# The LayerNorm apply of the QKV stage goes from GpSimd with four input slots to VectorE with two

## What is computed

```
q, k, v = ln(x) @ Wq.T, ln(x) @ Wk.T, ln(x) @ Wv.T      # 2048, 512, 512 columns; 8 kv heads, 4 queries each
a_dot   = softmax(q k^T / 8) v                            # 32 heads of 64
a_mem   = elu(q) @ memory / (elu(q) @ memory_norm)
out     = a_dot * (1 - w) + a_mem * w                     # w = sigmoid(memory_weight)
ffn(x)  = ((silu(ln(x) @ w_gate * s_gate) * (ln(x) @ w_up * s_up)) @ w_down) * s_down   # int8 weights, 8192 inner
ln(x)   = (x - mean(x)) / sqrt(var(x) + 1e-5)
```

## Time and profile before

| | us |
|---|---|
| runs shown (2): median | 3299.47 |
| runs shown: lowest, highest | 3222.3, 3376.64 |
| the profiled execution, device time | 3150.48 |
| its span on the slowest core (4) | 3148.8 |
| spans of the eight cores | 3109.7 to 3148.8 |

### The profile page before, as it was taken

How to read it: one execution, slowest core, us unless ns; L and a number is a source line. 1 busy time by engine, 2 the same in 40 slices (tenths; PEclk the granted TensorE clock), 3 DMA queues, 4 the chain that set the end, 5 groups by cost and what they waited for, 6 DMA issues and landing times.

```text
span 3148.8 us, 40986 instructions; the slowest of 8 cores (3109.7 to 3148.8 us)
## 1 busy us (share of the span) xinstructions
PE 2460.3 (78%) x14265; PEld 1331.1 (42%) x14265; DVE 594.8 (19%) x1657; ACT 963.0 (31%) x1671; POOL 590.8 (19%) x1071
## 2 busy tenths in 40 slices
PE   3677667787844699968999778786449997899986
PEld 1232222122211477724777322221127775278752
DVE  1323332111136300020000011112460002010010
ACT  2200030899930122201222049996002221022210
POOL 1100010000000133323333310000003332333333
PEclk8788867788855799989999988887559998999999
DMA  5222113000000499979999970000009997999999
GB/s 142 71 43 47 38 59 84 23 4 4 3 2 1 151 360 355 359 274 360 356 351 356 354 255 4 4 4 3 1 1 360 355 350 251 395 352 361 346 332 346
DMA packets 161916, 591.77 MB, mean 188 GB/s; under 512 B 20920, under 2 KB 23096, under 8 KB 157368
## 3 DMA queue, kind: packets, MB, share of 16 engines
q0 software_dynamic: 151344, 552.14, 51.2%
q1 hardware_dynamic: 10376, 37.01, 3.4%
HBM read 325.23 MB, written 8.39 MB: 106 GB/s over the span
## 4 chain that ended last, share of the span: by engine, by line
PE 58%; DVE 12%; ACT 11%; DMA 11%; issue 8%; DVEq 1%; SPq 0%; POOL 0%; ACTq 0%; POOLq 0%
PE pAB L713 14%; PE pAB L704 14%; ACT arena L481 9%; DMA warena<-wd 8%; PE pCD L296 5%; PE pAB L296 5%; PE pCD L675 3%; PE pE L493 3%; PE pAB L461 3%; PE pF L493 2%; PE pAB L578 2%; PE pF L675 2%; PE pE L675 2%; PE pT L238 2%; DVE x L633 1%
## 5 line engine op out<-in xcount | busy, mean ns | idle before, releaser
L704 PE MATMUL pAB<-ln_fm,warena 128*128 128x256 bf16 x4096 | 493.5, 274 | 9.7 <-DMA warena<-wg 4.8
L713 PE MATMUL pAB<-ln_fm,warena 128*128 128x256 bf16 x4096 | 490.1, 273 | 9.9 <-DMA warena<-wu 6.3
L694 POOL DMA_DIRECT2D warena<-wg x256 | 136.2, 532 | 1733.6 <-PE pAB L704 1038.7
L704 PEld LDWEIGHTS pAB<-ln_fm,warena 128*128 128x128 bf16 x4096 | 398.0, 98 | 122.5 <-issue 39.1
L713 PEld LDWEIGHTS pAB<-ln_fm,warena 128*128 128x128 bf16 x4096 | 399.0, 98 | 63.6 <-issue 16.4
L481 ACT ACTIVATE arena<-pAB,bias_s 128x512 bf16<-128x512 f32 x512 | 372.0, 727 | 48.2 <-PE pCD L468 44.9
L481 ACT ACTIVATE arena<-pCD,bias_s 128x512 bf16<-128x512 f32 x512 | 374.3, 731 | 0.0
L461 PE MATMUL pAB<-q_fm,k_fm 64*128 64x512 bf16 x512 | 219.7, 439 | 131.7 <-ACT arena L481 126.7
L720 ACT ACTIVATE gtmp<-pAB,sg_s 128x256 bf16<-128x256 f32 x256 | 121.2, 473 | 566.0 <-PE pAB L713 505.2
L728 DVE TENSOR_TENSOR arena<-gtmp,utmp 128x256 bf16<-128x256 bf16 x256 | 74.8, 292 | 1061.7 <-ACT utmp L724 1061.7
L493 PE MATMUL pE<-arena,v_tm 128*65 128x512 bf16 x512 | 230.3, 450 | 0.0
(11 more groups left out here) (121 smaller groups left out, 2070.1 us busy)
## 6 DMA issues: line engine op xcount, KB each, us to landing
warena<-wd POOLq DMA_DIRECT2D x512, 512.0 KB, 6.0
warena<-wg POOLq DMA_DIRECT2D x256, 512.0 KB, 3.8
warena<-wu POOLq DMA_DIRECT2D x256, 512.0 KB, 4.7
x<-x SPq DMA_DIRECT2D x16, 1024.0 KB, 7.0
xstage<-x SPq DMA_DIRECT2D x8, 1024.0 KB, 5.0
warena<-wqt POOLq DMA_DIRECT2D x16, 512.0 KB, 5.2
y<-x SPq DMA_DIRECT2D x8, 1024.0 KB, 5.2
warena<-wkt POOLq DMA_DIRECT2D x8, 512.0 KB, 5.2
```

What stands on the lines that cost most here:

```text
L704: ttg = P.do("t", lambda e, it=it, wb=wb, c=c: e.matmul(pA[0:128, 0:256], wgb[wb][:, c, :], ln2_fm[:, c, 0:256], start=(c == 0), stop=(c = ...
L713: ttu = P.do("t", lambda e, it=it, wb=wb, c=c: e.matmul(pB[0:128, 0:256], wub[wb][:, c, :], ln2_fm[:, c, 0:256], start=(c == 0), stop=(c = ...
```

## The change

The apply of the QKV stage is issued on VectorE instead of GpSimd; the four input slots become the two halves of `xstage`; the waits of the later reloads of `x1` that guarded the two borrowed slots go. Places in the order of emission stay: stats(i), tail(i-1), apply(i). In the VectorE queue the apply of tile i thus stands behind V copy(i-1) and ahead of stats(i+1).

```diff
-        xslots = [xstage[:, 0, :], xstage[:, 1, :], x1[:, 2, :], x1[:, 3, :]]
-        xstreams = ["xs0", "xs1", "a2", "a3"]
-        war_xslot = [None] * 4
         for H in range(2):
             for i8 in range(8):
                 i = H * 8 + i8
                 sl = i % 2
-                s4 = i % 4
-                t_x[i] = P.do("y", lambda e, i=i, s4=s4: e.dma_start(
-                    out=xslots[s4], in_=x_d[i * 128:(i + 1) * 128, :]),
-                    waits=[war_xslot[s4]], stream=xstreams[s4])
-                tv3 = emit_ln_stats(xslots[s4], sl, [t_x[i]], war_lnst[sl],
+                t_x[i] = P.do("y", lambda e, i=i, sl=sl: e.dma_start(
+                    out=xstage[:, sl, :], in_=x_d[i * 128:(i + 1) * 128, :]),
+                    waits=[war_xstage[sl]], stream="xs%d" % sl)
+                tv3 = emit_ln_stats(xstage[:, sl, :], sl, [t_x[i]], war_lnst[sl],
                                     sum_on_s=True)
                 if i8 > 0:
                     emit_tile_tail(i - 1)
-                t_apply[i] = emit_ln_apply(xslots[s4], sl, tv3, eng="g")
-                war_xslot[s4] = t_apply[i]
+                t_apply[i] = emit_ln_apply(xstage[:, sl, :], sl, tv3, eng="v")
+                war_xstage[sl] = t_apply[i]
             emit_tile_tail(H * 8 + 7)
...
         t_sdb = P.do("y", lambda e: e.dma_start(out=xstage[:, 1, :], in_=sdb_d[:]),
-                     waits=[war_xslot[1]], stream="xs1")
+                     waits=[war_xstage[1]], stream="xs1")
...
-                xw = [t_y[loc]] if p == 1 else []
-                if p == 0:
-                    if loc == 0:
-                        xw = [P.lastj]
-                    elif loc >= 2:
-                        xw = [t_apply[12 + loc], war_lnst[loc % 2]]
                 t_x1.append(P.do("y", lambda e, p=p, loc=loc: e.dma_start(
                     out=x1[:, loc, :],
                     in_=x_d[p * 512 + loc * 128: p * 512 + (loc + 1) * 128, :]),
-                    waits=xw, stream="a%d" % loc))
+                    waits=[t_y[loc]] if p == 1 else
+                          ([P.lastj] if loc == 0 else []), stream="a%d" % loc))
```

## The result

| | before | after |
|---|---|---|
| median, us | 3145.38 (10 runs) | 3162.67 (11 runs) |
| lowest, highest, us | 3135.86, 3376.64 | 3157.5, 3403.88 |
| ratio | | 1.0067 (95% interval 1.0047 to 1.0086) |
| the profiled execution's span, slowest core | 3148.8 | 3176.4 |
| mean span of the eight cores, same execution | 3131.1 | 3158.8 |

A program on all eight cores has a second state in which a die runs at a lower granted clock; the two runs shown with the kernel before (3222.3 and 3376.64) were both in it, and the ratio leaves such runs out.

What follows compares the result with a forecast made beforehand. VectorE and TensorE taking turns on one chain was taken to bound the QKV stage. Exposed applies 21.5 plus head 2.4 gave 23.9, near 24 us; on the shown median 3299.5 that made 3323.5, range 3165 to 3400.

Steps and rivals of the forecast that it cites:

- The time stated: Whole kernel: 3323.5 us, from the shown runs' median 3299.5 plus 24; range 3165 to 3400.
- The middle tiles: QKV stage, six tiles a half: the apply exposed behind the V copy costs 1.45 us each, 12 times.
- The last tiles: Last tile of each half: no stats hide the first transposes, so copies start 2.05 us later, twice.
- The first tile of a half free: First apply of each half costs nothing: VectorE idles 3.9 us behind it for ScalarE's sums, against 1.35.
- Sum of the exposed applies: Both halves of the QKV stage: 12 x 1.45 + 2 x 2.05 = 21.5 us.
- The head: Start of the kernel: two earlier Q loads beside the first x loads delay it 2.4 us, bounds 0 and 5.
- The slots: x loads with two input slots instead of four: cost nothing, with about 11 us before VectorE feels a late load.
- Rival C: QKV loads late with two slots, each tile waiting for its x: slower by over 2%, 3366 us or more; chance 0.09.
- The clock: TensorE's V groups: 0 us taken, bounds -15 and +22, as changed groups would be like the typical one.
- Rival A: Longer pauses keep TensorE at 1.2 GHz through all V groups: +22, so +46 us, 3345; chance 0.14.
- Rival B: Apply hidden in VectorE's idle 6.1 us under the V group: only 2.4 us cost, 3302; chance 0.05.
- Rival D: Faster by over 2%, through something later in the program that shifts with the start; needs 66 us; chance 0.04.

Runs made afterwards that it cites:

- e7: Changed kernel with the apply not waiting for the V copy ahead of it on its own engine: no ratio; middle gap 3.41 us, halves 102.8 and 102.9 us.
- e5: Changed kernel with each apply of the QKV stage issued twice in a row: ratio 1.0161 to the kernel before.
- e1: Kernel before with only the QKV apply moved to VectorE, four input slots kept: ratio 1.0056 to the kernel before.
- e2: Changed kernel with the apply back on GpSimd, two slots kept: ratio 0.9996 to the kernel before.
- e6: Changed kernel with the load of x tile i+2 held until the last copy of tile i: ratio 1.0114 to the kernel before.
- e3: Changed kernel with the apply on VectorE emitted between the 16 copies and the V copy of the tile before: ratio 0.9994 to the kernel before.

## Why the prediction was right, and where it was wrong

**The time stated: wrong, at the step from the term to the total.** The sum against the profiled execution was 3150.5 + 24 = 3174.5, and that execution's counterpart took 3178.4. Such a close hit is luck in part: the latter lay 16 us above the median of its kernel, as core 0 took 3176.4 us and the other seven 3150 to 3162. With the medians it is 3145.4 + 24 = 3169 against 3162.7. For the time stated, though, the prediction took the median of the two runs shown, 3299.5, as the base. They lay 2.3% and 7.2% above the profiled execution. The prediction saw a gap of 4.7% to their median and let it stand as a spread, with the profiled execution as its edge. It was the reverse: of ten runs of before, six lie between 3135.9 and 3145.5, and the profiled execution was the ordinary one. The range inherited it: its low end was the profiled time plus 14 us, while ordinary runs lie some 5 us below that time. For the 14 the prediction gives no working, and its own lower bound for the change was 6. Even the sum on the right base, with bounds of 6 and 48 us, would have held the result: 3156 to 3198.

**The size and the sign: right.** Slower by 24 us was forecast; 15 to 27 were measured. By terms:

- *The middle tiles.* 12 times 1.45 was predicted; the gap grew by 1.49. Its three parts hold: 0.20 for the wait on the own engine (e7 took away 0.20), 1.35 for the instruction, the rest overlap.
- *The last tiles.* 2.05 predicted, 2.01 measured in the gap.
- *The first tile of a half free.* e5 fits: its middle gaps grew by 1.45 and the first V copy of half 0 kept its place (50.9 against 51.1 us on the mean of the cores), and that of half 1 came 24.0 us behind the K chunks, against 23.8.
- *Sum of the exposed applies.* 21.5 predicted, 12 x 1.49 + 2 x 2.01 = 21.9 in the gaps, 22.5 in the whole of the halves.
- *The head.* The 2.4 us were wrong; they measured 0. On the mean of the cores the first L194 started at 27.6 us against 27.4, the first V copy at 51.1 in both; in e1, with all four early x loads and the two early Q loads together, it came at 50.9. The delay itself was there, but at the second tile: on the mean of the cores the first x tile landed at 27.3 us before and 27.5 after, the second at 30.6 and 33.2, 2.6 us later. The step that failed was to put it on the path. ScalarE is at work on the first tile until then and starts the second L194 only at 34.1 before and 34.3 after, so on every core the second tile was there in time. On core 0 of after it landed at 36.1, and ScalarE went from the square root of the first tile to the sum of the second with no wait for a load:

```profile
36.53 0.20 ACT L216 ACTIVATE stat<-stat 128x1 f32<-128x1 f32 x1
36.88 1.91 ACT L194 ACTIVATE x<-xstage 128x2048 f32<-128x2048 f32 x1
```

  The Q loads were issued near 23 us as predicted (23.2 on the mean).
- *The slots.* Nothing, as predicted; e2 shows it and e6 shows the 11 us that the prediction gave a load. Rival C falls.
- *The clock.* 0 was taken, and the total bears it out, but not the reason given, that the changed V groups would be like the typical one. The granted clock did fall, above all in the copies (e5). And in half 1 short and long V groups now mostly take turns, as these two neighbours on core 0 of after show, with 0.69 and 0.56 of the clock:

```profile
423.86:429.28 5.42, 5.17 (x16) 1.88 (x16) 0.00 (x1) 3.89 (x4) 0.00 (x0) 0.69 0.00 0
438.36:445.05 6.69, 6.06 (x15) 2.21 (x16) 0.01 (x1) 3.89 (x4) 0.00 (x0) 0.56 0.00 0
```

  The middle V groups of after range from 5.06 to 6.71 us, those of before from 5.62 to 6.48. Their mean was 0.12 shorter and the copies 0.10 longer; at the last tiles the V groups were 0.22 longer. It nets out, and that the short and the long ones balance is luck as far as these runs show. Rival A falls for this change: its V groups at 1.2 GHz throughout did not come.
- *Hidden after all.* Rival B would have come true with another place in the queue, as e3 shows; with this one it falls.
- *Faster.* Rival D falls; no later stage gave anything back.

The rule of the Trainium skill that was laid beside the price (VectorE: DVE Perf Modes, the perf-mode tier table) gives 1227 ns; all sixteen applies in the QKV stage took 1345 to 1347 ns, so the measurement decides:

```profile
L224 DVE TENSOR_SCALAR lnstage<-xstage,stat x16: 1345/1346/1347, 37.1 to 505.5; 128x2048 bf16<-128x2048 f32 x16
```

## What to carry to other kernels

An engine's busy share does not say whether it has room; its idle time has a place. Here 1.35 us in VectorE's queue cost 1.5 us a tile behind the V copy and nothing 6 us earlier, and using that same idle time for the stats as well made the slowest core 0.5% faster than before. Ask of each instruction what stands ahead of it in its queue and what it waits for: if that is the end of another engine's long work, everything emitted behind it is paid for, so emit ahead of the wait whatever is ready. And choose the base of a stated time with as much care as the term: when the few runs shown lie well apart from the profiled execution, settle which of them is the ordinary one before adding to either.

## What had not been expected of the hardware

TensorE's granted clock fell with the change, from 0.75 to 0.67 between 47 and 140 us on the mean of the cores, and yet the V groups did not get longer on the mean (6.03 and 5.91 us). The fall lay in the copies, where the clock matters little, and the V groups spread to both sides. At the gap of 4.83 us of e6 they took 5.88, at the 5.06 of e5 they took 6.28; what it is in the pause that decides is not shown.

Two Q loads of 512 KB each, issued near 23 us while the first x tiles were under way, moved the landing of the first tile by 0.2 us and that of the second by 2.6, about as much as the x load issued beside two of them later on (7.4 us instead of 5.0). It cost nothing, as the second tile had more slack than that.
